# The two routed stages of a six-stage kernel are written anew: norm in halves, folded keys and value table, another order of work

## The chip, the cores and the metric

The kernel runs on one NeuronCore of a Trainium2 chip. The metric is the device time of one execution in microseconds (us), as the median of several runs. Engine names in the profile: PE is TensorE (PEld its weight loads), DVE is VectorE, ACT is ScalarE, POOL is GpSimd, SP issues the DMAs.

## The reference

A batch of 2 sequences of 512 tokens, 512 features wide, goes through six stages that each add to it: a quantized feed-forward, a state space layer ("mamba"), the feed-forward again, a routed stage, attention, and the routed stage once more. The change concerns the routed stage, which is applied twice with the same weights. It takes the layer norm `h` of x and computes:

```python
query = h @ Wq.T                                   # 512 -> 64
rq = query @ Wr.T;  rk = aux_keys @ Wr.T           # 64 -> 48, 128 slots
router_scores = rq . rk / sqrt(48) + log_rel
top_scores, top_idx = top_k(router_scores, 8)
attn = query . aux_keys[top_idx] / sqrt(64) + log_rel[top_idx]
w = softmax(attn)
aux_out = (w @ aux_values[top_idx]) @ Wvd.T @ Wvu.T    # 512 -> 32 -> 512
log_var = log1p(var(h));  norm_var = log_var / (mean(log_var) + 1e-06)
learned = gelu(h @ Wu1.T + bu1) @ Wu2.T + bu2
u = clip(norm_var * 0.5 + sigmoid(learned) * 2.5, 0, 5)
gate = sigmoid(gate_w1 * clip((u - 0.5) / 1.5, 0, 1) + gate_bias), 0 where below 0.05
x = x + 0.5 * (h + gate * aux_out)
```

All of it is float32.

## The kernel before

x stays in SBUF as 8 tiles of 128 tokens (`x`, [128, 8, 512]) from the first stage to the last. Stages follow one another: each opens a block in which every engine runs its own program, and the programs meet only at semaphores. At the end of a block all engines pass a barrier. No scheduler reorders anything: on each engine the order is that of the code.

A routed stage is two such blocks. The first is the shared function `norm_transpose`: VectorE takes the statistics of 8 tiles (L137, L140), POOL raises the variance to the power -0.5 (L181), VectorE normalizes (L145), TensorE transposes each tile in four 128x128 pieces (L221), ScalarE copies them to `hT` (L212). VectorE then takes statistics of the normalized tiles for `var` (L150 to L155). The second block begins with 13 DMAs for weights and vectors on SP (L469 to L476), and TensorE's first product waits for all of them.

In the second block TensorE makes the queries (L483), the router keys (L486), the product of values and Wvd (L488), the hidden units (L492) and router queries (L497). It then makes for each of 8 token tiles a router score and an attention score (L507, L508) in banks that VectorE empties two at a time. VectorE works on all 8 tiles in turn: the 8 largest router scores of a token (`max`), `match_replace` to mark them, and four passes that make a mask and a penalty from the marks (L587 to L601), then the maximum (L604). ScalarE makes the exponentials (L557). VectorE divides the weights by their sum (L614). After the learned term (L515) TensorE transposes the weights (L522), multiplies by the 32-column table (L527) and by WvuT (L533), in two banks that VectorE empties with the last add (L640). The gate's chain of small operations (L617 to L634) and the residual (L636) lie before the first add.

In the names of the profile, `routed_hT` is tile hT of either routed stage. `Chain.link` gives an instruction a semaphore and waits for it; `Chain.step` only counts.

## Time and profile before

| | us |
|---|---|
| median of 3 runs | 2702.19 (2700.91 to 2704.57) |
| profiled execution | 2699.94 |
| its span in the profile | 2698.1 |
| TensorE busy | 2403.2 (89%) |
| VectorE busy | 1718.1 (64%) |
| ScalarE busy | 1302.0 (48%) |
| GpSimd busy | 1332.2 (49%) |

The span runs from the first to the last instruction recorded. Busy shares are means over six unlike stages; the mean granted clock of TensorE is 0.941 of its full rate, where 1.00 is 2.4 GHz and 0.50 is 1.2 GHz. Of the span, the first routed stage begins near 2149 us and the second near 2594 us.

### The profile page before, as it was taken

To read this page: it belongs to the slowest core of one execution; us is meant where nothing else is said; L and a number is where in the kernel's file an instruction comes from. 1 tells how busy PE (TensorE), PEld (TensorE's weight loads), DVE (VectorE), ACT (ScalarE), POOL (GpSimd) and SP (SyncE) were. 2 spreads that over 40 slices of the span, in tenths; PEclk is the share of its full clock that TensorE was granted. 3 is DMA by queue.
4 is the path that set the end of the run, shared out by engine and by line. 5 is a ranking of instruction groups with operands and counts; after the bars stand their busy time and mean duration, and the time that the engine had idled before them with its cause. 6 is when DMAs were issued, how large, how long until landed. Compare 5 with 4: busy or idle time off the path is not lost. (4 is left out here: it accounts for less than half of the span.)

```text
span 2698.1 us, 32843 instructions
## 1 busy us (share of the span) xinstructions
PE 2403.2 (89%) x12160; PEld 1851.6 (69%) x12160; DVE 1718.1 (64%) x2342; ACT 1302.0 (48%) x1884; POOL 1332.2 (49%) x877
## 2 busy tenths in 40 slices
PE   4995699999999999999999999998699857889955
PEld 3873578778778778788788788786477633566623
DVE  4554578578588588588588588585456345664325
ACT  2311467467467467477477477475232022235521
POOL 1222189579589489489499499497222100000000
PEclk9997799999999999999999999998799967999986
DMA  3420333233223233233233233231153002000000
GB/s 98 102 84 5 99 98 110 86 98 110 86 94 110 90 95 118 82 104 115 75 106 110 78 106 110 75 106 60 36 116 97 27 14 73 1 2 2 2 14 31
DMA packets 163542, 204.12 MB, mean 76 GB/s; under 512 B 24408, under 2 KB 86360, under 8 KB 163256
## 3 DMA queue, kind: packets, MB, share of 16 engines
q1 hardware_dynamic: 163384, 202.02, 24.9%
q8 instruction: 98, 1.61, 0.2%
q14 instruction: 60, 0.49, 0.1%
HBM read 198.49 MB, written 3.15 MB: 75 GB/s over the span
## 5 line engine op out<-in xcount | busy, mean ns | idle before, releaser
L1601 POOL TENSOR_TENSOR mamba_w_lo<-mamba_raw,mamba_w_hi 128x512 fp32r<-128x512 f32 x272 | 435.1, 1608 | 293.5 <-ACT mamba_w_hi L1465 293.5
L76 PE MATMUL psum<-mamba_hT_lo,mamba_w_hi 128*128 128x512 f32 x1152 | 461.9, 401 | 6.3 <-POOL mamba_w_lo L1601 6.3
L77 PE MATMUL psum<-mamba_hT_hi,mamba_w_hi 128*128 128x512 f32 x1152 | 456.3, 396 | 0.0
L78 PE MATMUL psum<-mamba_hT_hi,mamba_w_lo 128*128 128x512 f32 x1152 | 456.3, 396 | 0.0
L1620 POOL TENSOR_SCALAR mamba_L<-mamba_A,mamba_ts 128x256 f32<-128x256 f32 (+1 forms) x256 | 333.0, 1315 | 0.1
L1718 DVE TENSOR_TENSOR mamba_L<-mamba_L,mamba_cb 128x1536 f32<-128x1536 f32 x128 | 309.0, 2414 | 21.8 <-ACT mamba_L L1514 13.9
L1686 DVE SCALAR_TENSOR_TENSOR mamba_hid<-psum,mamba_cw,mamba_hid 128x1022 f32<-128x1022 f32 (+2 forms) x192 | 245.1, 1277 | 21.4 <-ACT mamba_hid L1472 16.8
L76 PEld LDWEIGHTS psum<-mamba_hT_lo,mamba_w_hi 128*128 128x128 f32 x1152 | 217.0, 188 | 56.6 <-POOL mamba_w_lo L1601 6.7
L78 PEld LDWEIGHTS psum<-mamba_hT_hi,mamba_w_lo 128*128 128x128 f32 x1152 | 217.0, 188 | 52.5
L77 PEld LDWEIGHTS psum<-mamba_hT_hi,mamba_w_hi 128*128 128x128 f32 x1152 | 217.2, 189 | 49.2
L350 POOL TENSOR_TENSOR ffn_w_lo<-ffn_deq,ffn_w_hi 128x512 fp32r<-128x512 f32 (+2 forms) x66 | 84.3, 1277 | 298.0 <-ACT ffn_w_hi L360 298.0
L1745 DVE SCALAR_TENSOR_TENSOR mamba_zs_lo<-mamba_z,mamba_dgn,mamba_zs_hi 128x512 fp32r<-128x512 f32 x128 | 117.2, 920 | 175.3 <-ACT mamba_zs_hi L1537 175.3
L1703 DVE SCALAR_TENSOR_TENSOR mamba_L<-mamba_A,mamba_ts,mamba_zero 128x256 f32<-128x256 f32 (+1 forms) x512 | 215.6, 488 | 11.5 <-DMA mamba_A<-mamba_a_dram 11.5
L76 PE MATMUL psum<-mamba_w_lo,mamba_zs_hi 128*128 128x512 f32 x512 | 205.7, 402 | 14.0 <-DVE mamba_zs_lo L1745 13.1
L77 PE MATMUL psum<-mamba_w_hi,mamba_zs_hi 128*128 128x512 f32 x512 | 203.5, 397 | 0.0
L78 PE MATMUL psum<-mamba_w_hi,mamba_zs_lo 128*128 128x512 f32 x512 | 203.3, 397 | 0.0
L1537 ACT ACTIVATE mamba_zs_hi<-mamba_z,mamba_dgn 128x512 fp32r<-128x512 f32 x128 | 91.6, 722 | 192.1 <-PE psum L78 192.1
L1465 ACT CAST mamba_w_hi<-mamba_raw 128x512 fp32r<-128x512 f32 x272 | 165.8, 610 | 36.1 <-PE psum L78 25.8
L181 POOL TENSOR_TENSOR routed_n_rstd<-routed_n_ve,s_nhalf 128x8 f32<-128x8 f32 x2 | 3.3, 1639 | 361.4 <-DVE routed_n_ve L142 361.4
L1472 ACT ACTIVATE mamba_hid<-psum,mamba_cw 128x1024 f32<-128x1024 f32 x64 | 77.2, 1206 | 202.4 <-PE psum L78 202.4
L1369 PE MATMUL psum<-mamba_L,mamba_hc 128*64 128x256 f32 x1024 | 159.7, 391 | 3.7 <-DVE mamba_L L1718 3.7
L76 PE MATMUL psum<-ffn_hT_lo,ffn_w_hi 128*128 128x512 f32 (+1 forms) x352 | 139.5, 396 | 24.6 <-POOL ffn_w_lo L350 24.6
(286 smaller groups left out, 5040.8 us busy)
## 6 DMA issues: line engine op xcount, KB each, us to landing
mamba_A<-mamba_a_dram SPq DMA_DIRECT2D x128, 512.0 KB, 4.6
mamba_raw<-in_win SPq DMA_DIRECT2D x144, 256.0 KB, 2.6
mamba_raw<-in_wout SPq DMA_DIRECT2D x128, 256.0 KB, 2.6
mamba_Eb<-mamba_e_dram SPq DMA_DIRECT2D x128, 128.0 KB, 3.0
ffn_raw<-in_w SPq DMA_DIRECT2D x80, 128.0 KB, 3.5
ffn_scl<-in_s SPq DMA_DIRECT2D x80, 128.0 KB, 3.8
ffn_scl<-in_s SPq DMA_DIRECT2D x86, 64.0 KB, 2.3
ffn_raw<-in_w SPq DMA_DIRECT2D x20, 256.0 KB, 2.6
```

Of the source, the lines that this page charges most:

```text
L76: e.matmul(out, wh, ml, start=start, stop=False)
L77: e.matmul(out, wh, mh, start=False, stop=False)
L78: return e.matmul(out, wl, mh, start=False, stop=stop)
L1369: e.matmul(psum[lo:lo + HD, 5 + b, q:q + HALF], hc[:, token_tile(b, c, 0), lo:lo + HD], L[:, m % 3, c, h, 0:HALF], start=True, stop=False)
L1465: e.copy(w.hi[:, k % NSPLIT, :], raw[:, k % NRAW, :]).then_inc(s["w_hi"], 1)
L1537: e.activation(zs.hi[:, q % 2, :], z[:, i, p, :], ACT.Copy, scale=dgn[:, grp, i, 1:2]).then_inc(s["z_hi"], 1)
L1601: e.tensor_tensor(w.lo[:, k % NSPLIT, :], raw[:, k % NRAW, :], w.hi_read[:, k % NSPLIT, :], ALU.subtract).then_inc(s["w_lo"], 1)
L1620: last = e.tensor_scalar(out, A[:, m % 2, h, lo:SEQ], ts[:, token_tile(b, 1, j), 1, head], 0.0, ALU.subtract, ALU.min)
L1686: ins = e.scalar_tensor_tensor(t[:, :, k:], banks(kind, n)[:, :, :SEQ - k], cw[:, grp, i, 3 - k:4 - k], t[:, :, k:], ALU.mult, ALU.add)
L1703: last = e.scalar_tensor_tensor(out, A[:, m % 2, h, lo:hi], ts[:, token_tile(b, c, j), 1, head], zero[:, 0:1].to_broadcast([P, hi - lo]), ...
L1718: e.tensor_tensor(t, t, cb[:, m % 2].unsqueeze(2).to_broadcast([P, 2, 2, WCOL]), ALU.mult).then_inc(s["m_ready"], 1)
L1745: e.scalar_tensor_tensor(zs.lo[:, q % 2, :], z[:, i, p, :], dgn[:, grp, i, 1:2], zs.hi_read[:, q % 2, :], ALU.mult, ALU.subtract).then_inc ...
```

## The change

Only `routed_ffn` is edited. It no longer calls `norm_transpose`; the norm is in its own single block. Statistics and the power run by halves of four tiles (POOL also sets a row of ones in `qT`). The DMAs, now 14, are issued by SP at the start of that block. The variance of the normalized tile is worked out from the first statistics (var times rstd squared) in two small operations.

The router keys are folded with Wr into one 64x128 matrix, so that both scores of a tile come from the query alone; `log_rel` is added by a 65th row, against the row of ones. Router score and attention score of a tile are one product with 256 columns. The value table is folded too: `vv` is values by Wvd by Wvu, [128, 512], and a token tile's output is one product with 128 rows. The softmax's division and the gate are one factor applied in the last add. The residual is done by ScalarE from x itself, with per-token scale and offset. GELU's square moves to ScalarE; the hidden units and tanh run by halves; the constant 0.5 of GELU moves behind the product. Selection uses one penalty pass over four tiles, and the maximum is one reduction over four tiles. The output uses four banks.

The core of the diff:

```diff
-        norm_transpose(nc, g, name + "n_", hT, xn, var_out=var)
...
+        def score_bank(h, i):
+            return (4, 0)[h] + i // 2
+        def scores(h, part):
+            n = (4, 0)[h]
+            return g["psum"][:, n:n + 2, :].rearrange("p b (t s n) -> p (b t) s n", t=2, s=2)[:, :, part, :]
...
+                for dst, src in small:
+                    e.dma_start(dst[:], d[src]).then_inc(w_in, 16)
                 for dst, src in loads:
                     e.dma_start(dst[:], d[src].rearrange("(a p) n -> p a n", p=P)).then_inc(w_in, 16)
-                for dst, src in small:
-                    e.dma_start(dst[:], d[src]).then_inc(w_in, 16)
-                e.dma_start(lrel[:], d["lrel"].partition_broadcast(P)).then_inc(w_in, 16)
+                for n in range(2):
+                    e.dma_start(keys[BOT:BOT + 1, n, :], d["lrel"].unsqueeze(0)).then_inc(w_in, 16)
...
+            @block.gpsimd
+            def _(e):
+                e.memset(qT[BOT:BOT + 1, :], 1.0).then_inc(row_set, 1)
+                e.wait_ge(row_set, 1)
+                for h in range(2):
+                    e.wait_ge(var_ready, h + 1)
+                    e.tensor_tensor(rstd[:, half(h)], ve[:, half(h)], nhalf[:, 0:NH_T], ALU.pow
+                                    ).then_inc(rstd_ready, 1)
...
+                def score(h):
+                    e.wait_ge(q_sb, h + 1)
+                    for i in range(NH_T):
+                        t = h * NH_T + i
+                        last = e.matmul(ps[score_bank(h, i)][:, i % 2 * 2 * NSLOT:(i % 2 + 1) * 2 * NSLOT],
+                                        qT[:, t * P:(t + 1) * P], keys[:].rearrange("p s n -> p (s n)"),
+                                        start=True, stop=True)
+                    last.then_inc(s_mm, 1)
...
+                def value(t):
+                    e.wait_ge(t_sb, t // NH_T + 1)
+                    if t >= len(OUT):
+                        e.wait_ge(o_used, t - len(OUT) + 1)
+                    e.matmul(ps[OUT[t % len(OUT)]], wT[:, t * P:(t + 1) * P], vv[:], start=True, stop=True
+                             ).then_inc(o_mm, 1)
+                for t in range(NT):
+                    turn(t)
                 e.wait_ge(w_in, NL)
+                e.transpose(ps[7][0:RDIM, 0:BOT], WrT[:], ident[0:BOT, 0:BOT])
+                e.matmul(ps[7][0:RDIM, P:P + NSLOT], WrT[:], akT[:], start=True, stop=True)
+                for a in range(DT):
+                    last = e.matmul(ps[7][0:VB, 3 * P:3 * P + NSLOT], WvdT[:, a, :], avT[:, a, :], start=a == 0,
+                                    stop=a == DT - 1)
+                last.then_inc(vd_mm, 1)
+                e.wait_ge(t_used, NT)
+                query(0)
+                e.wait_ge(wr_sb, 1)
+                e.wait_ge(rk_sb, 1)
+                e.matmul(ps[4][0:BOT, 0:NSLOT], Wr[:], rkT[:], start=True, stop=True).then_inc(g_mm, 1)
+                e.wait_ge(vd_sb, 1)
+                e.matmul(ps[5], vdT[:], WvuT[:], start=True, stop=True).then_inc(vv_mm, 1)
+                query(1)
+                e.wait_ge(row_set, 1)
+                e.wait_ge(ak_sb, 1)
+                e.wait_ge(g_sb, 1)
+                e.wait_ge(vv_sb, 1)
+                score(0)
+                score(1)
+                hidden(0)
+                hidden(1)
+                e.wait_ge(q_sb, 2)
+                turn_weights(0)
+                e.wait_ge(lvr, 1)
+                e.matmul(ps[2][:, NT:NT + 1], ones[:], lvs[:], start=True, stop=True).then_inc(lv_mm, 1)
+                e.wait_ge(u_sb, 2)
+                for t in range(NH_T // 2):
+                    value(t)
+                e.wait_ge(gelu, 2)
+                e.wait_ge(lv_used, 1)
+                for t in range(NT):
+                    last = e.matmul(ps[2][:, t:t + 1], u3[:, t * P:(t + 1) * P], sc[:, 1:2], start=True, stop=True)
+                last.then_inc(lr_mm, 1)
+                for t in range(NH_T // 2, NH_T):
+                    value(t)
+                turn_weights(1)
+                for t in range(NH_T, NT):
+                    value(t)
...
+                def residual(h):
+                    for t in range(h * NH_T, (h + 1) * NH_T):
+                        e.activation(x[:, t, :], x[:, t, :], ACT.Identity, scale=ra[:, t:t + 1], bias=rb[:, t:t + 1]
+                                     ).then_inc(resid, 1)
...
+                e.wait_ge(var_set, 1)
+                e.activation(lv[:], var[:], ACT.Ln, bias=1.0, accum_out=lvs[:]).then_inc(lvr, 1)
...
+                take_query(0)
+                e.wait_ge(g_mm, 1)
+                e.activation(keys[0:BOT, 0, :], ps[4][0:BOT, 0:NSLOT], ACT.Identity,
+                             scale=RDIM ** -0.5).then_inc(g_sb, 1)
+                e.wait_ge(vv_mm, 1)
+                e.copy(vv[:], ps[5]).then_inc(vv_sb, 1)
+                take_query(1)
+                take_scores(0)
+                take_scores(1)
+                e.wait_ge(affine, 2)
+                residual(0)
+                evacuate(0)
+                exponentials(0)
+                tanh(0)
+                take_weights(0)
+                evacuate(1)
+                exponentials(1)
+                tanh(1)
+                e.wait_ge(z1, 1)
+                e.activation(s1[:], s1[:], ACT.Exp, scale=-1.0).then_inc(ez1, 1)
+                take_weights(1)
+                e.wait_ge(z2, 1)
+                e.activation(gate[:], gate[:], ACT.Exp, scale=-1.0).then_inc(ez2, 1)
+                residual(1)
...
+                def pick(h):
+                    tiles = range(h * NH_T, (h + 1) * NH_T)
+                    e.wait_ge(rs_sb, h + 1)
+                    for t in tiles:
+                        ch.step(e.max(out=top[:, t, :], in_=rs[:, t, :]))
+                    ch.wait()
+                    for t in tiles:
+                        ch.step(e.match_replace(out=rep[:, t, :], in_to_replace=top[:, t, :], in_values=rs[:, t, :],
+                                                imm_value=-3.0e38))
+                    ch.wait()
+                    e.tensor_scalar(rep[:, half(h), :], rep[:, half(h), :], -2.0e38, -BIG, ALU.is_gt, ALU.mult
+                                    ).then_inc(pen_set, 1)
+                    e.wait_ge(pen_set, h + 1)
+                    e.tensor_tensor(at[:, half(h), :], scores(h, 1), rep[:, half(h), :], ALU.add
+                                    ).then_inc(at_set, 1)
+                    e.wait_ge(at_set, h + 1)
+                    e.tensor_reduce(nmx[:, half(h)], at[:, half(h), :], AX.X, ALU.max, negate=True
+                                    ).then_inc(peaked, 1)
+                def factor(h):
+                    e.wait_ge(exped, (h + 1) * NH_T)
+                    ch.link(e.reciprocal(rden[:, half(h)], den[:, half(h)]))
+                    e.tensor_tensor(fac[:, half(h)], gate[:, half(h)], rden[:, half(h)], ALU.mult
+                                    ).then_inc(fac_set, 1)
+                def add(h):
+                    e.wait_ge(fac_set, h + 1)
+                    for t in range(h * NH_T, (h + 1) * NH_T):
+                        e.wait_ge(o_mm, t + 1)
+                        e.wait_ge(resid, t + 1)
+                        e.scalar_tensor_tensor(x[:, t, :], ps[OUT[t % len(OUT)]], fac[:, t:t + 1], x[:, t, :],
+                                               ALU.mult, ALU.add).then_inc(o_used, 1)
...
+                for h in range(2):
+                    for t in range(h * NH_T, (h + 1) * NH_T):
+                        ch.step(e.bn_stats(st[:, t, :], x[:, t, :]))
+                    ch.wait()
+                    for t in range(h * NH_T, (h + 1) * NH_T):
+                        ch.step(e.bn_aggr(mv[:, t, :], st[:, t, :]))
+                    ch.wait()
+                    e.tensor_scalar(ve[:, half(h)], mv[:, half(h), 1], EPS, None, ALU.add).then_inc(var_ready, 1)
...
+                for h in range(2):
+                    e.wait_ge(rstd_ready, h + 1)
+                    for t in range(h * NH_T, (h + 1) * NH_T):
+                        e.tensor_scalar(xn[:, t, :], x[:, t, :], mv[:, t, 0:1], rstd[:, t:t + 1],
+                                        ALU.subtract, ALU.mult).then_inc(xn_ready, 1)
+                ch.link(e.tensor_tensor(vh[:], mv[:, :, 1], rstd[:], ALU.mult))
+                e.tensor_tensor(var[:], vh[:], rstd[:], ALU.mult).then_inc(var_set, 1)
+                e.tensor_scalar(ra[:], rstd[:], 0.5, 1.0, ALU.mult, ALU.add).then_inc(affine, 1)
+                e.scalar_tensor_tensor(rb[:], mv[:, :, 0], -0.5, rstd[:], ALU.mult, ALU.mult).then_inc(affine, 1)
+                e.wait_ge(w_in, NL)
+                pick(0)
+                gelu_in(0)
+                pick(1)
+                gelu_out(0)
+                gelu_in(1)
...
+                gelu_out(1)
...
+                factor(0)
+                add(0)
+                factor(1)
+                add(1)
```

TensorE, first routed stage, from the norm's transposes (`xn` by the identity `s_ident`) on; before:

```order
L221 MATMUL psum<-s_ident,routed3_xn 128x128 x32
L127 UNCONDITIONAL_BRANCH
L478 UNCONDITIONAL_BRANCH
L483 MATMUL psum<-routed3_hT,routed3_WqT 64x512 x8
L486 MATMUL psum<-routed3_akT,routed3_WrT 48x128
L488 MATMUL psum<-routed3_WvdT,routed3_avT 128x32 x4
L492 MATMUL psum<-routed3_hT,routed3_Wu1T 128x512 x8
L497 MATMUL psum<-routed3_qT,routed3_WrT 48x512 x2
L507 MATMUL psum<-routed3_rkT,routed3_rqT 128x128
L508 MATMUL psum<-routed3_akT,routed3_qT 128x128
```

and in the changed kernel:

```order
L504 MATMUL psum<-s_ident,routed3_xn 128x128 x32
L543 MATMUL psum<-s_ident,routed3_WrT 48x64
L544 MATMUL psum<-routed3_akT,routed3_WrT 48x128
L546 MATMUL psum<-routed3_avT,routed3_WvdT 32x128 x4
L514 MATMUL psum<-routed3_hT,routed3_WqT 64x512 x4
L553 MATMUL psum<-routed3_rkT,routed3_Wr 64x128
L555 MATMUL psum<-routed3_WvuT,routed3_vdT 128x512
L514 MATMUL psum<-routed3_hT,routed3_WqT 64x512 x4
L522 MATMUL psum<-routed3_keys,routed3_qT 128x256 x8
L509 MATMUL psum<-routed3_hT,routed3_Wu1T 128x512 x8
L530 MATMUL psum<-s_ident,routed3_at 128x128 x4
L568 MATMUL psum<-routed3_lvs,s_ones 128x1
```

The weight-only products now lie between transposes and queries (one query half each side of the folded keys and table), scores come ahead of the hidden units, and two branches between blocks are gone.

ScalarE in the same stage, from the logarithm (`lv`) on, before (and behind it, of the changed kernel, from the hidden units on):

```order
L552 ACT_TABLE_LOAD
L552 ACTIVATE routed3_lv,routed3_lvs<-routed3_var 128x8
L554 ACT_TABLE_LOAD
L554 ACTIVATE routed3_u3<-routed3_u3 128x1024
L557 ACTIVATE routed3_at,routed3_den<-routed3_at,routed3_mx 128x128 x8
L560 ACTIVATE routed3_s1<-routed3_s1 128x8
L562 ACTIVATE routed3_gate<-routed3_gate 128x8
L565 COPY routed3_wT<-psum 128x512 x2
L568 COPY routed3_lowT<-psum 32x512 x2
```

and in the changed kernel:

```order
L612 ACT_TABLE_LOAD
L612 ACTIVATE routed3_at,routed3_den<-routed3_at,routed3_nmx 128x128 x4
L594 ACTIVATE routed3_u2<-routed3_u2 128x512
L617 COPY routed3_wT<-psum 128x512
L587 ACTIVATE routed3_u<-psum,routed3_sc 128x512
L589 ACTIVATE routed3_u2<-routed3_u 128x512
L612 ACTIVATE routed3_at,routed3_den<-routed3_at,routed3_nmx 128x128 x4
L594 ACTIVATE routed3_u2<-routed3_u2 128x512
L650 ACTIVATE routed3_s1<-routed3_s1 128x8
L617 COPY routed3_wT<-psum 128x512
L653 ACTIVATE routed3_gate<-routed3_gate 128x8
L606 ACTIVATE s_x<-s_x,routed3_rb,routed3_ra 128x512 x4
```

The table load for exponentials now stands between the first square and the first exponentials, and the copy of half 1's weights (`wT`) between the two exponentials of the gate.

TensorE at the stage's end, from the sum of `lvs` on, before (and behind it, of the changed kernel, from the hidden units on):

```order
L512 MATMUL psum<-routed3_lvs,s_ones 128x1
L515 MATMUL psum<-routed3_sc,routed3_u 128x1 x8
L522 MATMUL psum<-s_ident,routed3_at 128x128 x8
L527 MATMUL psum<-routed3_wT,routed3_vd 32x512 x2
L533 MATMUL psum<-routed3_WvuT,routed3_lowT 128x512 x8
```

and in the changed kernel:

```order
L509 MATMUL psum<-routed3_hT,routed3_Wu1T 128x512 x8
L530 MATMUL psum<-s_ident,routed3_at 128x128 x4
L568 MATMUL psum<-routed3_lvs,s_ones 128x1
L537 MATMUL psum<-routed3_vv,routed3_wT 128x512 x2
L575 MATMUL psum<-routed3_sc,routed3_u3 128x1 x8
L537 MATMUL psum<-routed3_vv,routed3_wT 128x512 x2
L530 MATMUL psum<-s_ident,routed3_at 128x128 x4
L537 MATMUL psum<-routed3_vv,routed3_wT 128x512 x4
```

One value product of 512 columns per tile takes the place of two, and half of them stand behind the second half's weight transposes.

## Rows read from the trace of the kernel before

**Rows 1.** Stretches: us, busy of each engine (count), granted clock, DMA share, GB/s.
```profile
2244.00:2594.00 350.00, 306.75 (x1516) 193.86 (x1516) 173.70 (x266) 138.54 (x255) 4.82 (x6) 0.97 0.05 16
...
2650.00:2665.00 15.00, 0.11 (x1) 0.02 (x1) 14.48 (x75) 3.19 (x16) 0.00 (x0) 0.50 0.00 1
```

**Rows 2.** Timeline of both routed stages: start us, us, engine, line, operation.
```profile
2148.76 4.84 DVE L137 BATCH_NORM_STATS2 routed_n_st<-s_x 128x6 f32<-128x512 f32 x8 [0.82 <-PEq L53]
...
2243.30 0.75 DVE L640 SCALAR_TENSOR_TENSOR s_x<-psum,routed_gate,s_x 128x512 f32<-128x512 f32 x1 [0.96 <-PE psum L533]
...
2594.05 4.84 DVE L137 BATCH_NORM_STATS2 routed_n_st<-s_x 128x6 f32<-128x512 f32 x8 [0.95 <-PEq L53]
...
2599.86 1.64 POOL L181 TENSOR_TENSOR routed_n_rstd<-routed_n_ve,s_nhalf 128x8 f32<-128x8 f32 x1 [333.75 <-DVE routed_n_ve L142]
...
2601.53 3.74 DVE L145 TENSOR_SCALAR routed_xn<-s_x,routed_n_mv,routed_n_rstd 128x512 f32<-128x512 f32 x8 [1.76 <-POOL routed_n_rstd L181]
...
2608.15 1.22 ACT L212 COPY routed_hT<-psum 128x512 f32<-128x512 f32 x2 [0.17 <-PE psum L221]
...
2612.00 0.40 SPq L469 DMA_DIRECT2D routed_WqT<-in_rWqT  x1
...
2618.30 0.43 SPq L476 DMA_DIRECT2D routed_sc<-in_gate_bias  x1
...
2621.16 9.87 PE L483 MATMUL psum<-routed_hT,routed_WqT 128*64 128x512 f32 x16 [12.42 <-DMA routed_sc<-in_gate_bias]
...
2688.64 0.75 DVE L640 SCALAR_TENSOR_TENSOR s_x<-psum,routed_gate,s_x 128x512 f32<-128x512 f32 x1 [0.96 <-PE psum L533]
```

**Rows 3.** Stretches of TensorE at either clock, both stages.
```profile
2163.00:2164.50 1.50, 0.76 (x6) 0.42 (x4) 1.50 (x4) 1.28 (x3) 0.00 (x0) 1.00 0.00 0
...
2175.80:2178.00 2.20, 2.15 (x3) 0.75 (x4) 0.00 (x0) 0.00 (x0) 0.00 (x0) 0.50 0.00 0
...
2180.00:2182.00 2.00, 2.00 (x6) 0.61 (x5) 0.00 (x0) 0.58 (x1) 0.00 (x0) 1.00 0.00 0
...
2235.00:2244.00 9.00, 8.26 (x10) 2.46 (x8) 4.22 (x6) 0.00 (x0) 0.00 (x0) 0.50 0.00 0
...
2645.00:2650.00 5.00, 5.00 (x23) 4.61 (x21) 2.81 (x12) 0.78 (x1) 0.00 (x0) 0.50 0.02 3
```

**Rows 4.** Timeline, TensorE's products in the second routed stage.
```profile
2633.60 5.74 PE L492 MATMUL psum<-routed_hT,routed_Wu1T 128*128 128x512 f32 x13
...
2643.85 0.74 PE L507 MATMUL psum<-routed_rkT,routed_rqT 48*128 48x128 f32 x2 [1.58 <-DVE routed_at L582]
...
2665.40 3.57 PE L515 MATMUL psum<-routed_sc,routed_u 128*128 128x1 f32 x16 [15.29 <-DVE routed_u L609]
...
2678.03 10.57 PE L533 MATMUL psum<-routed_WvuT,routed_lowT 32*128 32x512 f32 x12 [0.99 <-DVE s_x L640]
```

**Rows 5.** Groups of instructions on ScalarE: busy us, mean ns, idle before.
```profile
L557 ACT ACTIVATE routed_at<-routed_at,routed_mx 128x128 f32<-128x128 f32 x16 | 6.2, 388 | 30.2 <-DVE routed_mx L605 30.2
...
L547 ACT ACTIVATE routed_u<-psum,routed_sc 128x512 f32<-128x512 f32 x4 | 2.7, 687 | 12.2 <-PE psum L492 12.2
...
L552 ACT ACT_TABLE_LOAD x2 | 2.6, 1283 | 0.0
...
L552 ACT ACTIVATE routed_lv<-routed_var 128x8 f32<-128x8 f32 x2 | 0.4, 208 | 0.0
```

**Rows 6.** Timeline, VectorE and the gate in the second routed stage.
```profile
2650.15 1.65 DVE L587 MAX8 routed_top<-routed_rs 128x8 f32<-128x128 f32 x8
...
2651.91 0.28 DVE L590 MATCH_REPLACE8 routed_rep<-routed_top,routed_rs 128x128 f32<-128x128 f32 x1
...
2663.40 0.68 DVE L607 TENSOR_SCALAR routed_u<-routed_u 128x1024 f32<-128x1024 f32 x1
...
2671.10 0.21 ACT L562 ACTIVATE routed_gate<-routed_gate 128x8 f32<-128x8 f32 x1 [1.62 <-DVE routed_gate L629]
...
2672.19 4.90 DVE L636 SCALAR_TENSOR_TENSOR s_x<-routed_xn,s_x 128x512 f32<-128x512 f32 x8
```

272 lines of the change are left out of this document (102 added, 170 removed).

## The prediction

> **What bounds it now.** I began with the table of stretches [rows 1]. Attention, between the two routed stages, keeps TensorE busy for 306.75 of 350 us at a clock of 0.97; a routed stage is different: in one stretch of 15 us VectorE works alone (14.48 us) with TensorE at 0.11 us. So neither engine bounds a routed stage, its chain of dependent steps does, and what is read is where each step starts. The timeline [rows 2] gives both stages: from the first statistics at 2148.76 to the last add's end at 2243.30 + 0.75 = 2244.05, and from 2594.05 to 2688.64 + 0.75 = 2689.39: 95.3 us each. From here times are counted from a stage's first statistics. Nothing else is edited, so the forecast is the old time less twice what a stage loses.
>
> **Before, in three pieces** (second stage). Norm: normalizing starts at 7.5, the last hT copy ends at 2609.37 or 15.3, then come second statistics, a barrier, and the first weight DMA at 18.0; the first query product waits for the last DMA until 27.1 [rows 2]. Middle: queries, hidden, scores, to about 2650 or 55.6 (TensorE busy to the end of that stretch [rows 3]), then VectorE's selection alone to about 2665 or 71 [rows 1]. Tail: learned term, gate, two value products, adds, to 95.3.
>
> **After, the norm.** Statistics of eight tiles take 5.8 us, from 2594.05 until POOL starts at 2599.86; four take half and a link, some 3.0, so both halves are done at 6.1. POOL's power took 1.64 us for 8 columns; for 4 I bound it by 0 and 1.64, so the first is ready by 4.8 and the second by 7.8, under the normalizing of tiles 0 to 3 (6.1 to 8.0). Its memset of one partition lies before 3.0, when POOL has nothing else. Normalizing starts at 6.1, not 7.5. From there to the last hT copy the old stage took 2609.37 - 2601.53 = 7.84 us; the same 32 transposes and 8 copies follow, so I take 8.0: hT is whole at 14.1. If VectorE's work held POOL up until 8.0, the second power would end at 9.7 and tile 4 be ready at 10.3; TensorE needs it then anyway at some 0.93 us a tile. The 14 DMAs are issued from 0 at the old pace, 6.30 us from the first of 13 to the last, and 2.86 more until TensorE was released [rows 2]: all in by 10, four us before their first user. The weight wait costs nothing; the three small products after the transposes (6 products, about 1.5 us as before) end at 15.1. The first query product starts there instead of at 27.1: 12.0 us gained. It is the surest term.
>
> **Clock.** In the first stage the last transposes ran at 1.00, some 6 us after the first; after 12 us of waiting the queries began at 0.50 and reached 1.00 within 5 us [rows 3]. So continuous work from 6.7 carries 2.4 GHz into the queries. A rule speaks against this: the Trainium skill, TensorE: Matmul & The Clock Gate, PE-mode transpose, says that transposes don't engage the full clock. By that rule the queries would begin at 1.2 GHz; the trace disagrees (1.00 between 2163.0 and 2164.5, transposes alone).
>
> **Queries to hidden.** One fp32 product of 512 columns is two instructions, each 0.43 us at full clock (13 in 5.74 us) [rows 4]. Query 0: 8 instructions, 3.4 us, to 18.5. Folded router keys and value table: 0.2 + 0.9, to 19.6. ScalarE's small copies end near 16.7, so these don't wait; its query copy, after 0.2 us of latency, ends at 19.3. Query 1 to 23.1. Scores are 8 products of 256 columns, which no row shows; between 128 and 512 columns I take half of the latter, 16 instructions at 0.215 = 3.45 us, to 26.6. Hidden: 16 x 0.43 = 6.9, to 33.5. Gone are 16 score products of 128 columns, of which the third on waited for VectorE to free a bank [rows 4], and the router query products.
>
> **Selection, under that.** ScalarE copies half 0's scores at 25.1 to 25.6. VectorE: 4 max at 0.2 (8 in 1.65), 4 replacements at 0.26, one scalar operation of 512 at 0.4 (1024 in 0.68) [rows 6], one add out of PSUM at 0.75 (as L640) [rows 2], one reduction of 512, unseen, between those two, 0.7, and gaps: 3.9, to 29.5. ScalarE meanwhile does four residuals: unseen with two operand columns; with one, 0.69 [rows 5], overlapped 0.6 or, twice the operands, 0.8; I take 2.5 for all four, to 29.9. It takes u at 30.3, squares (0.65) to 31.6, loads the exponential table (1.28) to 32.9, makes 4 exponentials at 0.39 to 34.5 [rows 5]. Here the table load has no cover: before, it lay under VectorE's selection, now it is 1.3 us on the path, counted. The Trainium skill, ScalarE: Activation LUTs, What ACT_TABLE_LOAD costs, puts 1.38 us of drain on top. By that rule each stage is 1.4 us longer; the trace disagrees, with 0.0 idle before the load and 0.0 before the Ln behind it.
>
> **Tail.** Four weight transposes, 0.5 and latency, to 35.3; copy, to 35.9; u half 1 and square, to 37.2; VectorE, having waited for the square behind which half 1's cube is queued, finished selecting half 1 at 36.2. Exponentials of half 1 to 38.8, tanh 39.4, last hidden value 40.1. TensorE has had 2 to 3 us of work in the 6.7 us since 33.5. Before, a gap of 1.58 us ahead of the third score pair [rows 4] was followed by 0.50 for the rest of them [rows 3], so I take 1.2 GHz here. The 16 instructions of the learned term: 3.57 us as before [rows 4], to 43.8. Value tiles 2 and 3: 4 instructions at 0.85, to 47.2; weight transposes at the norm's cold pace of 0.93 for four, to 48.1. The gate reaches its second exponential 0.3 + 0.2 + 1.6 after 43.8, at 45.9, but on ScalarE that stands behind the copy of half 1's weights, which waits for those transposes: 48.3 to 48.9. Gate exponential (its wait of 1.62 is that 1.6) and four links, 1.1 (2671.10 to 2672.19) [rows 6], to 50.0; factor 0.4. Adds start at 50.4. Value tile 4 needs tile 0's bank, so starts at 51.25; four tiles at 1.71 (12 instructions in 10.57 us include waits, 0.85 each) put tile 7's product at 56.4; its add starts 2.05 later and takes 0.75: 59.2. VectorE has done its adds before; residuals of half 1 end at 52.7.
>
> **Sum.** 95.3 - 59.2 = 36.1 a stage, 72.2 for two. Profiled time 2699.9 (span 2698.1) gives 2627.7; the median shown, 2702.2, stands 2.3 above it and gives 2630.0. The split: 12 up to the queries; 28.5 from the first query to the last score becomes 11.5, less 6.9 for the hidden product that now stands behind the scores, 10; the rest, some 14, from the selection by wide instructions under it, the missing second value product, four output banks.
>
> **Rivals.**
> Warm tail. The value products now contract 128 rows, where the 32-row ones ran 11 to 15 us back to back at 0.50 [rows 3, 4] while 128-row queries rose within 5 us. If TensorE holds 2.4 GHz from 33.5 on: learned term 1.8, two tiles 1.7, transposes 0.4 put the copy at 44.3 and the adds at 46.4; then VectorE's eight adds at 0.75 and a second factor bound it: 52.8. Saved 2 x 42.5 = 85: 2617. Against: the gaps, and the learned term's 1-column products, which showed no rise before.
> Cold middle. Scores contract 65 rows and the table 32; if the clock falls there, scores cost 3.45 more and hidden 2 more, all on the path: 64.7, saved 61: 2641. For it: the old scores, of 48 and 64 rows, stayed at 0.50 from 2645 to 2650. Against: they came after a gap; here full-size queries stand before them.
> Cold start: if the clock rises only with the queries, their first 5 us run at half rate, 2.5 lost, and 0.7 in the small products: 3.2 a stage, 2636. Against: the 1.00 in the transposes. The Trainium skill's sentence on transposes, above, would have it so.
> Dear switch: if the load on the path brings a second stretch as long as itself, 1.28 a stage, 2633. Against: no idle time beside either load. The Trainium skill's drain, above, is of that size.
> Slower: the clock stays at 1.2 GHz into attention, because the routed stage leaves TensorE as sparse as before but attention starts on it sooner. Attention has 306.75 us of TensorE work at 0.97; every us of it run at half rate adds about one, so this decides from 72 us on, and 100 us would give 2730. Against: the old stage also left at 0.50 and attention still shows 0.97.
> That the change doesn't do what it says (loads not early) I exclude: SP has the DMAs first in the block and no wait ahead.
>
> **Chances.** Forecast 0.54, warm tail 0.20, cold middle 0.18, cold start 0.02, dear switch 0.03, slower 0.02, no difference (all of it given back) 0.01. Within the forecast, unseen operands and latencies are worth +-2.5 us a stage, the clock's phase in the last tiles +-1: its own range is 2623 to 2637. To hold 8 in 10, both clock cases go in with their spread: 2612 to 2647. Two per mille, 5.4 us, is about what this kernel's timing can tell from no change; faster 0.97, same 0.01, slower 0.02.
>
> **What would show it.** First query product about 15 us into the stage at clock 1.00, no DMA ahead of it; last score near 26.6; a table load with both other engines waiting near 32; a second gap near 36 to 40; PEclk 0.50 through the learned term; ScalarE's gate exponential directly behind the weight copy; stage length 59. Wrong would be a query start beyond 17, a stage over 65, or VectorE as the releaser of the last adds. Attention should keep its length; if not, the clock rival holds.

## The result, and the profile after

The changed kernel took 2625.33 us (median of 4 runs, 2618.72 to 2627.59) against 2703.38 us for the kernel before beside it (4 runs, 2700.91 to 2704.96): a ratio of 0.9708, 95% interval 0.9689 to 0.9728. The forecast was 2630.0, in a range of 2612 to 2647. On another chip the pair gave 2625.36 and 2702.28, ratio 0.9718 (0.9705 to 0.9732). The profiled execution took 2625.93 us, with a span of 2624.1, 74.0 less than the span before.

The stages, each from its first statistics to the end of its last add:

| us | before | after | forecast |
|---|---|---|---|
| first routed stage | 95.29 | 57.26 | 59.2 |
| attention stage between them | 350.00 | 352.67 | as before |
| second routed stage | 95.34 | 57.06 | 59.2 |

So 38.0 and 38.3 us were saved where 36.1 each were forecast, 2.7 came back in attention, and the first stage began 0.46 us earlier; 38.0 + 38.3 - 2.7 + 0.5 = 74.1 us, which is the 74.0 between the spans but for rounding. Attention and the new counterpart of the 15 us that VectorE worked alone [rows 1], in the table of stretches:

```profile
2163.00:2182.70 19.70, 19.09 (x53) 8.43 (x52) 6.41 (x28) 11.20 (x27) 0.00 (x0) 1.00 0.00 1
...
2206.50:2558.00 351.50, 310.03 (x1516) 195.66 (x1516) 174.16 (x265) 138.75 (x255) 4.83 (x6) 0.96 0.05 15
```

Columns are as in [rows 1]. From the first query product to the end of the hidden layer TensorE is now busy for 19.09 of 19.70 us at full clock. VectorE's selection of the first half (2174.22 to 2178.18) lies under the hidden layer, which ends at 2182.08; that of the second half (2180.68 to 2184.63) only begins under it. Attention has the same 1516 instructions as before, but 3.28 us more of TensorE's busy time, at a clock of 0.96.

The timeline of the first routed stage answers to [rows 2, 4, 6]:

```profile
2148.26 0.51 SPq L478 DMA_DIRECT2D routed_WrT<-in_WrT  x1
2148.30 2.47 DVE L706 BATCH_NORM_STATS2 routed_st<-s_x 128x6 f32<-128x512 f32 x4 [0.82 <-PEq L53]
...
2151.54 1.01 POOL L494 TENSOR_TENSOR routed_rstd<-routed_ve,s_nhalf 128x4 f32<-128x4 f32 x1 [2.33 <-DVE routed_ve L711]
...
2154.29 3.74 DVE L715 TENSOR_SCALAR routed_xn<-s_x,routed_mv,routed_rstd 128x512 f32<-128x512 f32 x8
2154.46 1.32 POOL L494 TENSOR_TENSOR routed_rstd<-routed_ve,s_nhalf 128x4 f32<-128x4 f32 x1 [1.91 <-DVE routed_ve L711]
...
2154.75 0.43 SPq L486 DMA_DIRECT2D routed_sc<-in_gate_bias  x1
...
2161.54 0.59 ACT L621 COPY routed_hT<-psum 128x512 f32<-128x512 f32 x1 [0.22 <-PE psum L504]
...
2162.93 2.36 PE L514 MATMUL psum<-routed_hT,routed_WqT 128*64 128x512 f32 x5
...
2171.50 3.72 PE L522 MATMUL psum<-routed_keys,routed_qT 65*128 65x256 f32 x16
...
2174.22 0.87 DVE L675 MAX8 routed_top<-routed_rs 128x8 f32<-128x128 f32 x4 [15.77 <-ACT routed_rs L602]
...
2175.05 7.03 PE L509 MATMUL psum<-routed_hT,routed_Wu1T 128*128 128x512 f32 x16
...
2175.74 2.93 ACT L606 ACTIVATE s_x<-s_x,routed_rb,routed_ra 128x512 f32<-128x512 f32 x4
...
2179.41 0.63 ACT L589 ACTIVATE routed_u<-routed_u 128x512 f32<-128x512 f32 x1
2180.06 1.28 ACT L612 ACT_TABLE_LOAD   x1
...
2181.36 0.40 ACT L612 ACTIVATE routed_at<-routed_at,routed_nmx 128x128 f32<-128x128 f32 x1
...
2183.94 0.69 DVE L687 TENSOR_REDUCE routed_nmx<-routed_at 128x4 f32<-128x512 f32 x1
...
2185.05 2.83 PE L537 MATMUL psum<-routed_vv,routed_wT 128*128 128x512 f32 x4 [1.15 <-ACT routed_u L587]
...
2188.49 3.49 PEld L575 LDWEIGHTS psum<-routed_sc,routed_u 128*128 128x128 f32 x16 [2.19 <-DVE routed_u L668]
2188.49 3.57 PE L575 MATMUL psum<-routed_sc,routed_u 128*128 128x1 f32 x16 [0.62 <-DVE routed_u L668]
2191.93 3.76 PE L537 MATMUL psum<-routed_vv,routed_wT 128*128 128x512 f32 x4
...
2195.48 1.00 PE L530 MATMUL psum<-s_ident,routed_at 128*128 128x128 f32 x4
2196.52 0.59 ACT L617 COPY routed_wT<-psum 128x512 f32<-128x512 f32 x1 [3.94 <-PE psum L530]
2197.00 0.21 ACT L653 ACTIVATE routed_gate<-routed_gate 128x8 f32<-128x8 f32 x1
...
2197.24 0.17 DVE L745 TENSOR_SCALAR routed_gate<-routed_gate 128x8 f32<-128x8 f32 x1 [3.08 <-ACT routed_gate L653]
...
2198.50 2.73 DVE L701 SCALAR_TENSOR_TENSOR s_x<-psum,routed_fac,s_x 128x512 f32<-128x512 f32 x4
2199.40 5.37 PE L537 MATMUL psum<-routed_vv,routed_wT 128*128 128x512 f32 x8 [2.92 <-DVE s_x L701]
```

The reader is to see three things. The weight DMAs go out with the first statistics, and the first query product has no wait of its own behind a DMA; before, it had 12.42 us [rows 2]. The two waits of the tail are short and named: VectorE's 3.08 us for the gate's exponential, which stands behind the weight copy on ScalarE, and TensorE's 2.92 us for a bank that VectorE's first add frees. And the same kind of product takes 0.94 us an instruction at 2191.93 (3.76 for 4) but 0.67 at 2199.40 (5.37 for 8). The table of stretches, same columns, tells why:

```profile
2159.40:2163.00 3.60, 3.35 (x24) 2.38 (x25) 0.00 (x0) 3.14 (x5) 0.00 (x0) 1.00 0.00 0
...
2188.40:2191.90 3.50, 3.41 (x16) 3.41 (x17) 0.04 (x1) 0.00 (x0) 0.00 (x0) 0.50 0.00 0
2191.90:2195.50 3.60, 3.60 (x6) 1.43 (x7) 1.57 (x8) 0.21 (x1) 0.00 (x0) 0.50 0.00 0
2195.50:2199.40 3.90, 0.98 (x5) 0.67 (x4) 1.95 (x8) 2.88 (x6) 0.00 (x0) 0.90 0.00 0
2199.40:2202.00 2.60, 2.60 (x4) 1.14 (x5) 2.53 (x6) 0.62 (x1) 0.00 (x0) 0.56 0.00 0
2202.00:2205.00 3.00, 2.77 (x6) 0.86 (x4) 1.99 (x4) 0.00 (x0) 0.00 (x0) 0.81 0.00 0
```

The granted clock is 1.00 in the norm's last transposes and the small products, 0.50 through the learned term and tiles 2 and 3, 0.90 over the transposes and the wait behind them, back to 0.56 at the start of the last four tiles, and higher again (0.81) within them.

### The profile page after: what moved, and what is told of

Its sections match the earlier page's. It is cut to its first block and busy times, and to the rows that moved or that the text cites. A ratio compares the mean times of both kernels' runs of the same rounds, so it can differ in the third digit from the quotient of the medians.

```text
span 2624.1 us, 32587 instructions
## 1 busy us (share of the span) xinstructions
PE 2382.9 (91%) x12122; PEld 1842.2 (70%) x12122; DVE 1673.7 (64%) x2174; ACT 1316.2 (50%) x1910; POOL 1335.3 (51%) x881
## 5 line engine op out<-in xcount | busy, mean ns | idle before, releaser
L1829 DVE TENSOR_TENSOR mamba_L<-mamba_L,mamba_cb 128x1536 f32<-128x1536 f32 x128 | 308.9, 2413 | 22.0 <-ACT mamba_L L1625 14.1
L1814 DVE SCALAR_TENSOR_TENSOR mamba_L<-mamba_A,mamba_ts,mamba_zero 128x256 f32<-128x256 f32 (+1 forms) x512 | 215.4, 488 | 10.7 <-DMA mamba_A<-mamba_a_dram 10.7
```

The source lines that it names most:

```text
L1814: last = e.scalar_tensor_tensor(out, A[:, m % 2, h, lo:hi], ts[:, token_tile(b, c, j), 1, head], zero[:, 0:1].to_broadcast([P, hi - lo]), ...
L1829: e.tensor_tensor(t, t, cb[:, m % 2].unsqueeze(2).to_broadcast([P, 2, 2, WCOL]), ALU.mult).then_inc(s["m_ready"], 1)
```

## The experiments

Each kernel was profiled once; e9, e10 and e11 were run four or five times as well, and their stages below are those of the profiled execution (2613.25, 2614.59 and 2622.15 us). The kernel before took 2696.23 us beside e1 to e4, 2700.58 beside e5 to e8 and 2702.28 beside e9 to e12, each group on a chip of its own, so times of different groups are not to be held against each other closely. A verdict on a stage is read from the stage's length, not from the total: attention, which no edit touches, measured 350.0 to 355.4 us over these runs, with its clock, and that is as much as many of the edits are worth.

| kernel | time | routed stages | start of adds in them | attention |
|---|---|---|---|---|
| changed | 2625.93 | 57.26, 57.06 | 50.2, 50.0 | 352.67 |
| e1_late_loads | 2640.14 | 67.31, 66.76 | 58.9, 59.7 | 350.83 |
| e2_hidden_first | 2639.14 | 64.58, 64.59 | 57.5, 57.5 | 355.19 |
| e3_rows32 | 2626.43 | 59.38, 59.00 | 50.5, 50.2 | 351.02 |
| e4_early_table | 2620.28 | 54.19, 54.04 | 47.2, 47.0 | 354.45 |
| e5_fill | 2621.20 | 54.72, 55.01 | 49.0, 49.0 | 351.51 |
| e6_gate_first | 2613.44 | 51.73, 51.94 | 46.0, 45.9 | 354.36 |
| e7_early_turn | 2617.98 | 53.25, 51.90 | 46.2, 45.9 | 355.37 |
| e8_before_early | 2681.23 | 85.94, 84.66 | 74.0, 72.1 | 354.17 |
| e9_turn_table | 2613.62 (median) | 51.84, 51.83 | 45.0, 45.0 | 354.37 |
| e10_turn_table_fill | 2614.02 (median) | 50.87, 51.31 | 45.1, 45.3 | 354.12 |
| e11_after_again | 2625.36 (median) | 57.20, 55.53 | 50.1, 48.5 | 350.33 |
| e12_norm_whole | 2624.48 | 57.19, 57.31 | 50.1, 50.3 | 351.96 |

The theory was that the gain is the sum of the forecast's steps, each on one chain. The rival was that some of them are covered by others, so that undoing one costs nothing, and that what is left is the clock.

**e1_late_loads**: the weight DMAs wait for the transposed value again.

```diff
             def _(e):
+                e.wait_ge(t_used, NT)
                 for dst, src in small:
```

> The changed kernel, with the 14 DMAs of a routed stage held back until hT is whole. Times from a stage's first statistics; the changed kernel's stages are 57.3 and 57.1 us. If the early loads carry the first 12 us of the gain: DMAs issued from 13.9, landed by 23, first weight product at 23 instead of 13.1, first query product near 24.7 instead of 14.6, and it starts at clock 0.50, which costs 2 to 3 more; stage 68 to 70. If the gain up to the queries came from the norm in halves or from the missing barrier, and the weights were hidden anyway, the stage grows by at most 2.

Measured: +10.0 and +9.7 us, a little under the expected 11 to 13. The timeline of the first stage:

```profile
2158.27 0.51 SPq L479 DMA_DIRECT2D routed_WrT<-in_WrT  x1
...
2167.67 0.30 PE L544 MATMUL psum<-s_ident,routed_WrT 64*48 64x64 f32 x1 [10.04 <-DMA routed_sc<-in_gate_bias]
...
2170.33 1.97 PE L515 MATMUL psum<-routed_hT,routed_WqT 128*64 128x512 f32 x2
...
2183.61 7.03 PE L510 MATMUL psum<-routed_hT,routed_Wu1T 128*128 128x512 f32 x16
...
2204.17 6.69 PE L538 MATMUL psum<-routed_vv,routed_wT 128*128 128x512 f32 x8 [2.92 <-DVE s_x L702]
```

The stage began at 2144.33, so TensorE's first user of a weight stands at 23.3 us and the queries at 26.0, cold (two instructions in 1.97 us). The DMA wait is back. At fixed points it costs more than the stage's length shows: the queries start 11.4 and 11.3 us later in the two stages, the hidden layer 12.5 and 11.7, as expected. The tail gave some of it back by its clock: here the learned term ran warm in both stages (1.95 us), and tiles 2 and 3 took 1.96 and 3.41 where the changed kernel has 3.76. The early loads are worth some 12 us up to the hidden layer, of which 10 show in the stage.

**e8_before_early**: the same done alone, in the kernel before. Its 13 weight DMAs are issued at the start of the norm's block; nothing else is changed.

```diff
-        norm_transpose(nc, g, name + "n_", hT, xn, var_out=var)
...
+        def early(e):
+            for dst, src in loads:
...
+        norm_transpose(nc, g, name + "n_", hT, xn, var_out=var, sync=early)
...
         with nc.Block() as block:
-            @block.sync
-            def _(e):
-                for dst, src in loads:
```

> The kernel before, with one part of the change alone: the 13 DMAs of a routed stage are issued at the start of its norm block. Barrier and all else as before. If the wait for the loads was 9.1 us a stage (18.0 to 27.1): first query product at 17.5 to 18.3, stage 86 to 87 instead of 95.3, 17 to 18 us for both. If loads under the norm slow the norm, less.

Measured: the stages are 9.4 and 10.7 us shorter, 20 in both, where 17 to 18 were expected. The queries start at 18.0 us in each instead of 27.1, 9.1 earlier as expected; the second stage's further gain is the clock in them (16 instructions in 8.40 us instead of 9.87). So the loads pay by themselves, without the other edits. TensorE's query products then stand behind a barrier and not behind a DMA:

```profile
2163.90 2.79 PE L484 MATMUL psum<-routed_hT,routed_WqT 128*64 128x512 f32 x3 [2.84 <-PEq L53]
```

**e2_hidden_first**: the hidden layer in front of the scores.

```diff
-                score(0)
-                score(1)
                 hidden(0)
                 hidden(1)
+                score(0)
+                score(1)
```

> The changed kernel, with both hidden halves ahead of the scores on TensorE; nothing else moves. If scores first is what lets VectorE select under the hidden product, selection begins 6.9 later and with it the chain square, table, exponentials: stage +6.5 to +7, 64 us. If the order is neutral (the same products, and u could be taken earlier), within 1 us.

Measured: +7.3 and +7.5 us, a little over the 6.5 to 7 expected. The gap before the weight transposes is 7.78 us where it was 1.06:

```profile
2185.50 1.09 PE L530 MATMUL psum<-s_ident,routed_at 128*128 128x128 f32 x4 [7.78 <-ACT routed_at L612]
```

These transposes stand 6.8 and 6.9 us later than in the changed kernel, which is what was expected. The rest is the clock, 0.50 from there on: value tiles 0 and 1 took 3.78 us in both stages where the changed kernel has 2.83 and 3.07. The cover of the selection by the hidden layer is worth 6.8 us a stage.

**e3_rows32**: the value product contracts 32 of the 128 rows, as the old one did. It leaves out 96 of the 128 slots of each tile.

```diff
-                    e.matmul(ps[OUT[t % len(OUT)]], wT[:, t * P:(t + 1) * P], vv[:], start=True, stop=True
+                    e.matmul(ps[OUT[t % len(OUT)]], wT[0:32, t * P:(t + 1) * P], vv[0:32, :], start=True, stop=True
```

> The changed kernel, with the 8 value products contracting 32 of the 128 slots (96 slots are left out of the output); columns and instruction count stay. If the 128-row products are what raised the clock in the last four tiles (8 instructions in 5.37 us), these now stay at 0.50 and take 6.8 to 7: stage +1.5 to +1.9. If any continuous work raises it, no change (within 0.3).

Measured: +2.1 and +1.9 us, all but 0.3 and 0.2 of it behind the start of the adds:

```profile
2197.71 7.16 PE L537 MATMUL psum<-routed_vv,routed_wT 32*128 32x512 f32 x8 [2.92 <-DVE s_x L701]
```

Eight instructions take 7.16 us with 32 rows and 5.37 with 128: the same columns, the same waits, but the clock stays low, as it did for the old kernel's last tiles [rows 3, 4]. From 2184 to 2206 the granted clock was 0.50 throughout, the stretch ahead of the last tiles included, where the changed kernel had 0.90. With 128 rows the same eight instructions stand behind the same wait of 2.92 or 2.93 us in twelve stages of these runs: they took 5.28 to 5.37 us in eleven, and 6.69 in one, e1's first, at a clock of 0.54. So the rise within the last four tiles, which the forecast's sum didn't have, came with the fuller contraction, but the fuller contraction doesn't always bring it as early.

**e4_early_table**: an exponential of one column behind the logarithm, so that the table is loaded while TensorE makes the queries.

```diff
                 e.activation(lv[:], var[:], ACT.Ln, bias=1.0, accum_out=lvs[:]).then_inc(lvr, 1)
+                e.activation(early[:], var[:, 0:1], ACT.Exp)
```

> The changed kernel, with an exponential of one column right behind the logarithm on ScalarE, so that the table is loaded there (where ScalarE waits 2.26 us for the first query) and not between the first square and the first exponentials. If the load on the path costs its 1.28 us: everything from the exponentials on 1.3 earlier, stage 55.9. If it brings a drain as well: 2.6 earlier. If something else is late there (selection of half 0 ends at 29.9, exponentials start 33.1), less than 1.

Measured: -3.1 and -3.0, more than the load's 1.28 us. The load now stands under the queries, and the exponentials follow the square at once, at 31.6 us into the stage instead of 33.1. The learned term starts 0.9 and 0.7 us earlier. The surplus is the clock: the learned term took 1.95 us instead of 3.57.

```profile
2161.54 1.28 ACT L626 ACT_TABLE_LOAD   x1
...
2177.74 0.39 ACT L613 ACTIVATE routed_at<-routed_at,routed_nmx 128x128 f32<-128x128 f32 x1
...
2185.40 1.95 PE L576 MATMUL psum<-routed_sc,routed_u 128*128 128x1 f32 x16 [1.84 <-DVE routed_u L670]
```

**e6_gate_first**: the gate's exponential ahead of the copy of the second half's weights.

```diff
-                take_weights(1)
                 e.wait_ge(z2, 1)
                 e.activation(gate[:], gate[:], ACT.Exp, scale=-1.0).then_inc(ez2, 1)
+                take_weights(1)
```

> The changed kernel, with the gate's second exponential ahead of the copy of half 1's weights on ScalarE. If the gate waits behind that copy: it runs at 45.9 instead of 48.7, adds start at 47.3 instead of 50.2, value tile 4 at 48.9 (weights copied by then) instead of 51.1: stage 54.9 to 55.4. If TensorE's last tiles are set by the weight copy alone, within 0.3 of 57.2.

Measured: -5.5 and -5.1, against 1.8 to 2.3 expected from the order alone.

```profile
2183.99 2.05 PE L575 MATMUL psum<-routed_sc,routed_u 128*128 128x1 f32 x16 [1.46 <-DVE routed_u L668]
...
2188.17 0.21 ACT L652 ACTIVATE routed_gate<-routed_gate 128x8 f32<-128x8 f32 x1 [1.62 <-DVE routed_gate L743]
...
2190.57 3.69 PE L537 MATMUL psum<-routed_vv,routed_wT 128*128 128x512 f32 x8 [0.68 <-ACT routed_wT L617]
```

The exponential now waits only for its own input (1.62). The rest is the clock: the learned term took 2.05 us, the last eight instructions 3.69, although TensorE's order up to the learned term is the changed kernel's, word for word. So the level in the learned term isn't set by the edit, which lies behind it. The level in the last tiles may be: the wait ahead of them shrank from 2.92 us to 0.68.

**e7_early_turn**: the second half's weights transposed ahead of the learned term, and copied ahead of both gate exponentials.

```diff
+                turn_weights(1)
                 e.wait_ge(gelu, 2)
...
-                turn_weights(1)
...
+                take_weights(1)
                 e.wait_ge(z1, 1)
...
-                take_weights(1)
```

> The changed kernel, with the weight transposes of half 1 ahead of the learned term on TensorE and their copy ahead of the learned term's exponential on ScalarE. Both had 3 to 4 us of waiting there. Expected: gate exponential at 45.9, adds from 47.3, value tile 4 at 48.1: stage 54 to 54.5. If the transposes push the learned term back instead (they wait for half 1's exponentials, done 1.4 us before the hidden values), up to 0.5 is lost and the stage is 54.7. If the gate's place is not what binds, within 0.5 of 57.2.

Measured: -4.0 and -5.2, against 2.8 to 3.3 expected. The two stages of one execution differ by 1.35 us, and by the clock alone: the learned term took 2.33 and 1.95 us, tiles 2 and 3 1.96 and 3.66, the last tiles the reverse, 5.37 and 3.67.

```profile
2193.91 5.37 PE L537 MATMUL psum<-routed_vv,routed_wT 128*128 128x512 f32 x8 [2.71 <-DVE s_x L701]
...
2602.19 3.67 PE L537 MATMUL psum<-routed_vv,routed_wT 128*128 128x512 f32 x8 [1.01 <-DVE s_x L701]
```

The bank for the last tiles comes free at nearly the same time in both, so the stage that was quicker in tiles 2 and 3 waits longer ahead of the last ones, 2.71 us against 1.01. Over all runs with 128 rows the last eight instructions took 3.67 to 3.70 us behind a wait of at most 1.01 us (e5, e6, this stage), and 5.28 or more behind one of 2.71 to 2.93. The two go together; that the wait is the cause was not tried by itself.

**e5_fill**: extra products of 512 columns, whose results nothing uses, in the three gaps of the tail: one, two and three. Ahead of the first TensorE also waits for the selection of the second half, which frees the bank that they write.

```diff
+                e.wait_ge(at_set, 2)
+                fill(1)
                 for t in range(NH_T // 2):
                     value(t)
+                fill(2)
...
                 turn_weights(1)
+                fill(3)
```

> The changed kernel, with extra products of 512 columns into a free bank (results unused): 1 before value tile 0, 2 before the learned term, 3 before value tile 4, so that TensorE doesn't wait. If the tail is slow because of the clock: learned term at 1.00 in 1.8 us instead of 3.5, value tiles 2 and 3 in 1.75 instead of 3.6, adds start near 46.6, then VectorE's eight adds bound it: stage 52 to 54. If the learned term is bound by its weight loads at any clock, it stays 3.5 and the stage is 57 to 58, since the extra products only stand in the way.

Measured: -2.5 and -2.1. It did hold the clock from the learned term on, which took 1.84 us, with the last eight instructions at 3.67; tiles 0 and 1, behind the first extra product, took 3.50 and 3.46. But the extra products stand ahead of work that is ready, and give part of it back; the expected 3 to 5 was too much.

**e11_after_again**: the changed kernel once more, beside e9 and e10.

> The changed kernel itself, unaltered, on the same chip as e9 and e10. Both theories expect 2618 to 2628 us and a ratio to the kernel before of 0.970 to 0.973. It tells two things: whether the clock in the learned term and the last four tiles (0.50 and then 1.00 in the profile of the changed kernel) comes out the same in another execution, stages of 57.2 us again, or 55 to 59 if it varies by execution; and how far attention's length (352.67 us) varies with nothing changed, 350 to 355 expected.

Measured: 57.20 and 55.53 us in the two stages. The first repeats the earlier profile. In the second the learned term ran warm:

```profile
2188.46 3.58 PE L575 MATMUL psum<-routed_sc,routed_u 128*128 128x1 f32 x16 [0.50 <-DVE routed_u L668]
...
2596.46 1.95 PE L575 MATMUL psum<-routed_sc,routed_u 128*128 128x1 f32 x16 [1.46 <-DVE routed_u L668]
```

The same program, the same instructions ahead: in three of four stages the clock had fallen by the learned term, in one it had not. In the warm one the clock changed later against the stage: it reached 1.00 in the norm's transposes 12.4 us in and fell at 43.1, where the other three had 10.1 to 10.4 and 37.4 to 37.7. What decides that stays open. Its attention stage:

```profile
2205.50:2555.80 350.30, 306.83 (x1516) 193.97 (x1516) 173.73 (x265) 138.60 (x255) 4.86 (x7) 0.97 0.05 16
```

That is 350.33 us with TensorE busy for 306.83, the kernel before to a third of a us [rows 1]. So the 2.7 us that attention gave back in the first profile are no fixed price of the change. Whether attention is a little longer on average behind the changed kernel stays open, since the kernel before has one profile.

**e12_norm_whole**: one pass of statistics and one power for all eight tiles, instead of two halves.

```diff
-                for h in range(2):
-                    e.wait_ge(var_ready, h + 1)
-                    e.tensor_tensor(rstd[:, half(h)], ve[:, half(h)], nhalf[:, 0:NH_T], ALU.pow
-                                    ).then_inc(rstd_ready, 1)
+                e.wait_ge(var_ready, 2)
+                e.tensor_tensor(rstd[:], ve[:], nhalf[:, 0:NT], ALU.pow).then_inc(rstd_ready, 2)
...
```

> The changed kernel with the halves of the statistics joined: all 8 tiles' statistics, then one power over all 8, then the normalizing; all else as it is. Theory (the first half's normalizing is on the chain that sets when queries start): statistics of the second half, 8 passes of 0.6 us or so and the small operations, come ahead of the first normalizing; by the rows of the changed kernel the normalizing starts some 4 to 5 us later, and the second half's some 1 us earlier, so the queries, which need both halves, start 0 to +1.5 us later, and the stage is 57.2 to 58.7 us. Rival (the transposes and their evictions pace this part, and the halves let them start early): the whole delay of the first half shows, stage +3 to +4. Rival (the halves buy nothing, since the queries wait for the second half anyway and that comes earlier by the power it no longer waits for): stage -1. Time 2624 to 2634.

Measured: 57.19 and 57.31 us, which looks like nothing. But normalizing started 7.66 us into the stage instead of 5.99. The expectation had 4 to 5 us here, which was wrong: in the changed kernel too VectorE takes the second half's statistics ahead of the first normalizing. What the halves hide is GpSimd's power, 1.64 us:

```profile
2152.47 1.64 POOL L493 TENSOR_TENSOR routed_rstd<-routed_ve,s_nhalf 128x8 f32<-128x8 f32 x1 [5.08 <-DVE routed_ve L708]
2154.14 3.74 DVE L712 TENSOR_SCALAR routed_xn<-s_x,routed_mv,routed_rstd 128x512 f32<-128x512 f32 x8 [1.85 <-POOL routed_rstd L493]
...
2183.34 0.63 PE L528 MATMUL psum<-s_ident,routed_at 128*128 128x128 f32 x4 [1.07 <-ACT routed_at L610]
...
2188.69 1.95 PE L573 MATMUL psum<-routed_sc,routed_u 128*128 128x1 f32 x16 [1.47 <-DVE routed_u L666]
```

The weight transposes stand at 36.86 us into the stage where the changed kernel has 34.85, and the learned term at 42.2 for 40.2: 2.0 later (2.2 in the second stage), where 0 to 1.5 was expected. It ran warm in both stages and gave 1.6 of this back. Against the one warm stage of e11 (55.53) the second stage is 1.8 longer. So the halves are worth some 2 us, which the lengths alone would have hidden.

**e9_turn_table**: e7's order and e4's early load together. The edit is the two diffs above. The text below, put down before the run, names the step moved by e7 wrongly: what stands earlier are the transposes of the second half's weights and their copy, and nothing of the norm.

> The changed kernel with two of its steps moved together: the first half's normalizing and transposes stand ahead of the second half's statistics (as in e7_early_turn), and the table of the exponential is loaded at the routed stage's start (as in e4_early_table). Theory (the two savings are on one chain and add): by the rows, 3.0 for the order and 1.3 for the load, so a stage of 57.2 - 4.3 = 52.9 us where the learned term runs at the lower clock level, and about 51 where it runs at the upper; adds start 45 to 46.5. Span 2611 to 2617. Rival (the saving of the earlier load in e4 was the clock, 1.6 of its 3.0 us, and the same clock gain was already in e7): stages of 51.9 to 53.3 less only 1.3, 50.6 to 52. Rival that they don't add (something else, the hidden layer's evictions, ends last): stage 52 to 53, no better than e7. Time 2612 to 2618; attention's length may vary by some 5 us either way, as it did in all the runs.

Measured: stages of 51.84 and 51.83 us, and 2613.62 us (4 runs, 2612.35 to 2616.18) against 2625.36 for the changed kernel on the same chip (5 runs, 2622.15 to 2626.64): 11.7 less, and no run of the one within the runs of the other. Ratio to the kernel before 0.9676 (0.9662 to 0.9689). The adds start at 45.0 us, 0.9 before e7's second stage, in which the learned term was warm as well; the load's full 1.28 isn't added. That the second half's exponentials now wait 0.26 us for VectorE explains a part of this:

```profile
2180.85 0.40 ACT L613 ACTIVATE routed_at<-routed_at,routed_nmx 128x128 f32<-128x128 f32 x1 [0.26 <-DVE routed_nmx L689]
...
2190.29 5.17 PE L538 MATMUL psum<-routed_vv,routed_wT 128*128 128x512 f32 x8 [1.75 <-DVE s_x L703]
```

At the stage's end nothing of the 0.9 is left against e7's second stage (51.90), since the last eight instructions took 5.17 and 5.15 us here and 3.67 there. With a warm learned term 51 was expected.

**e10_turn_table_fill**: e9 with one extra product at each of three places, and e5's wait ahead of the first. The second place, which the text below calls the transposes of the normalized value, is behind the transposes of the second half's weights.

> e9_turn_table with one extra 512-column product, whose result nothing uses, at three places of each routed stage: before the first value tile, after the transposes of the normalized value, and before the fourth-last value tile. Theory (the clock of the last 10 us depends on what TensorE did before; a product in each gap holds it at the upper level): both stages alike at 50.5 to 52 us, learned term's products 1.8 to 2.0 us for the group rather than 3.57, last eight products 3.7 rather than 5.4; 1 to 2 us a stage below e9 where e9's are cold, nothing where they are warm. Rival (the extra products stand in the way, as they did in e5_fill, where each took 0.2 to 0.4 us ahead of work that was ready): a stage equal to e9's or up to 1 us longer. Span 2609 to 2616.

Measured: 50.87 and 51.31 us, 0.5 to 1.0 less than e9, with the last tiles at full clock in both stages, behind a wait of 1.85 us; in e9 a wait of 1.75 went with 5.17:

```profile
2193.66 3.67 PE L542 MATMUL psum<-routed_vv,routed_wT 128*128 128x512 f32 x8 [1.85 <-DVE s_x L711]
```

The time is e9's, 2614.02 (2610.9 to 2615.77): one us or two are too few to be seen in it. e9 and e10 beat both kernels; e6, with one line moved, came out at 2613.44 in its one run, on another chip.

## Why the prediction was right, point by point

Times from the first statistics, the forecast's and those of the changed kernel's first stage:

| step | forecast | measured |
|---|---|---|
| normalizing starts | 6.1 | 6.0 |
| hT whole | 14.1 | 13.8 |
| first query product | 15.1 | 14.6 |
| scores end | 26.6 | 26.9 |
| hidden layer ends | 33.5 | 33.8 |
| first exponentials end | 34.5 | 34.6 |
| last hidden value | 40.1 | 40.1 |
| learned term ends | 43.8 | 43.8 |
| tiles 2 and 3 end | 47.2 | 47.4 |
| gate exponential starts | 48.9 | 48.7 |
| adds start | 50.4 | 50.2 |
| stage ends | 59.2 | 57.3 |

**The norm and the early loads.** The query start moved from 27.1 to 14.6 us: 12.5 for the 12.0 worked out. The runs split it: 9.1 for the DMAs, from e8, where they alone move; 2.0 for the halves, from e12; the remaining 1.4 (the barrier and the second statistics that are gone, less the small products that now stand ahead) no run separates.

**The middle.** Every step is within 0.5 us. That rested on the clock of 2.4 GHz carried from the transposes into the queries: 1.00 from 2159.4 to 2163.0, in transposes and small products, and 1.00 up to 2182.7. The cold middle and the cold start did not come. The Trainium skill, TensorE: Matmul & The Clock Gate, PE-mode transpose, would have had the queries begin at half clock; the trace after disagrees as the one before did.

**The table load on the path.** It cost 1.28 us, from 2180.06, and the first exponential began 0.02 after it ended: the dear switch did not come. The Trainium skill, ScalarE: Activation LUTs, What ACT_TABLE_LOAD costs, puts a drain of 1.38 us on top; no idle time of that size stands on either side of this load.

**The tail up to the adds.** Cold, as forecast, in this profile; but e11 shows that the same program can be warm there: one of its four profiled stages was. The warm tail was a nearer rival than its 0.20 says. It came in full in none of the four, but the learned term was warm in both stages of e1, e4, e6 and e12, and in one of e7's (1.95 us, 2.33 in the other). These change nothing in TensorE's list of products ahead of it but when they start or, in e7, four transposes.

**The step that was mis-sized** is "four tiles at 1.71": the last four value tiles. Taken were 6.85 us for 8 instructions at the low clock, measured 5.37, since the clock rose within them. That is 1.5 of the 1.9 us between 59.2 and 57.3; 0.2 more came from the earlier start of the adds, and the rest from a shorter way from the last product to its add. The forecast had priced these 128-row products by the 32-row rows [rows 4], and e3 shows that with 32 rows it would have been right (7.16 for eight, stages of 59.4 and 59.0). The sentence that 128-row queries rose within 5 us [rows 3] stood in the forecast, under a rival, and was not used where 128-row products followed each other again.

**Attention** gave back 2.7 us in the profile, which the forecast excluded. It isn't the rival of a clock that stays low: TensorE has 1516 instructions in each, and its length less its busy time is 43.2 before (350.00 - 306.75) and 42.6 after (352.67 - 310.03). That rival would show at attention's start, and there nothing changed: in its first 40 us TensorE was busy for 26.7 us before and 26.6 after. The difference stands later, the last 20 of its first 350 us having 14.55 us at 1.00 before and 15.59 at 0.91 after. The length goes with the clock, up to 355.4, in kernels that don't differ there, and the changed kernel itself had 350.33 the second time.

**The total.** The profiled execution was 1.8 us under the sum of 2627.7: 4.1 more saved in the stages, 2.3 of it given back elsewhere. That the two partly cancel is luck. The other 2.9 us from 2630.0 to the median 2625.33 are how the profiled executions stand to the medians: 2.3 below before, 0.6 above after.

**Where the 38 us went.** 12.5 up to the first query product, as split above; 6.8 for the hidden layer over the selection (e2, at the weight transposes); 2 for the full contraction, through the clock of the last tiles (e3). The other 17 or so (selection by wide instructions, no second value product, four output banks, folded tables, fewer products ahead of the scores) were not tried one by one: that they come from these is argued from the steps in the timeline, not shown by a run. No step that was undone came free, so for these the rival, that others cover them, is out. The forecast cut the sum at other places, 12, 10 (with the folded keys in it) and 14, so the pieces can't be compared one by one.

## What to carry to other kernels

Write a sparse stage down as one chain, with a start time for each step, and look for the step whose wait is for something that could have been asked for earlier: the first DMA, the table, a copy that stands behind another engine's work. Price a matmul by rows with the same number of contraction rows, and give every tail with gaps in TensorE both clock levels. When an edit is worth a few us, read it at fixed points inside the stage, since the clock elsewhere moves the total, and even the stage's end, by as much.

## What the runs showed of the hardware that was not expected

- The granted clock at one place of one program differs between two stages of an execution, and between executions: sixteen instructions of the learned term in 3.58 or 1.95 us (e11), last tiles in 5.37 or 3.67 (e7). Stage length varied by 1.3 to 1.7 us from it. In e7 the wait ahead of the last tiles differed as well, 2.71 and 1.01 us.
- Weight loads of 128 columns follow the clock too: the learned term is bound by them (busy 3.49 of 3.57 us at 0.50, and 1.86 of 1.95 at 1.00 in e11, for products of one column).
- Behind the same wait, eight instructions of 512 columns took 7.16 us with 32 contraction rows in both stages of e3, the clock staying at 1.2 GHz; with 128 rows they took 5.28 to 5.37 us in eleven stages, the clock having risen, and 6.69 in one (e1).
- GpSimd's power took 1.01 and 1.32 us on 4 columns and 1.64 on 8: halving the work doesn't halve the time. ScalarE's residual with a scale and a bias column took 0.73 us a tile (2.93 for 4), against 0.59 for the plain copy out of PSUM of the same size.
